# A gated cross-attention and MoE layer: two halves of the head stack, re-dealt and re-ordered

## The reference, cut to what matters

```python
# x, ctx: (32, 128, 128) f32; D = 128, H = 16 heads of DH = 8
q, k, v    = split_heads(layernorm(x) @ Wqkv + bqkv)
_, ka, va  = split_heads(ctx @ Wqkv_aux + bqkv_aux)
p  = softmax(q @ k.T / sqrt(8));  pa = softmax(q @ ka.T / sqrt(8))
out = (p @ v) * (1 - sigmoid(g)) + (pa @ va) * sigmoid(g)      # per head
x = x + tanh(g_xattn) * (merge_heads(out) @ Wo + bo)
# then a mixture of 64 experts, 8 chosen per token, and a shared one
x = x + tanh(g_ffn) * moe(layernorm(x))
```

## Time and profile before

| | |
|---|---|
| median of the runs | 859.26 us |
| the profiled execution: time, span | 859.58 us, 857.8 us |
| PE, DVE, ACT, POOL busy, share of the span | 96%, 80%, 66%, 74% |
| attention, start to the first block | 0 to 36.4 us |
| attention, blocks | 36.4 to about 289 us |
| experts | about 289 us to the end |

### The profile page before, as it was taken

How to read it: one execution, slowest core, us unless ns; L and a number is a source line. 1 busy time by engine, 2 the same in 40 slices (tenths; PEclk the granted TensorE clock), 3 DMA queues, 4 the chain that set the end, 5 groups by cost and what they waited for, 6 DMA issues and landing times.

```text
span 857.8 us, 20206 instructions
## 1 busy us (share of the span) xinstructions
PE 826.2 (96%) x6733; PEld 646.0 (75%) x6733; DVE 683.6 (80%) x1648; ACT 566.8 (66%) x964; POOL 637.3 (74%) x602
## 2 busy tenths in 40 slices
PE   4899999999999999999999999999999999999997
PEld 3477777777766678888888888878888888888885
DVE  6789999999897769769678877867966977876665
ACT  4388888888878665575576576557557557655554
POOL 2668888888854378877787786777777788778785
PEclk8599999999999999999999999999999999999999
DMA  4677786776652167447456554654654755546562
GB/s 119 173 169 173 178 183 155 187 169 170 160 126 51 53 152 169 120 111 184 117 142 147 131 142 125 154 135 109 163 139 111 171 130 134 149 116 150 137 138 58
DMA packets 108036, 120.04 MB, mean 140 GB/s; under 512 B 28560, under 2 KB 70352, under 8 KB 106496
## 3 DMA queue, kind: packets, MB, share of 16 engines
q1 hardware_dynamic: 105056, 118.23, 57.5%
q10 hardware_dynamic: 2880, 0.59, 0.4%
HBM read 103.55 MB, written 14.71 MB: 138 GB/s over the span
## 4 chain that ended last, share of the span: by engine, by line
PE 87%; DVE 5%; DMA 3%; issue 2%; SPq 1%; ACT 1%; POOL 0%; DVEq 0%; POOLq 0%
PE bank L1999 20%; PE bank L2000 20%; PE bank L2001 20%; PE bank L1336 7%; PE bank L1323 5%; PE bank L1294 3%; PE bank L1276 2%; PE bank L1344 2%; PE bank L1260 1%; PE bank L1357 1%; DVE mx L989 1%; PE bank L1270 1%; DMA cwb<-wts_scratch 1%; DMA stack_q<-nmaxT 1%; PE bank L1976 1%
## 5 line engine op out<-in xcount | busy, mean ns | idle before, releaser
L1676 POOL TENSOR_TENSOR hid<-act,cwb 128x512 f32<-128x512 f32 x264 | 424.0, 1615 | 126.4 <-DVE act L1903 69.1
L1729 ACT ACTIVATE silu<-bank 128x512 f32<-128x512 f32 x256 | 152.9, 597 | 190.7 <-PE bank L2001 189.9
L1903 DVE TENSOR_TENSOR act<-silu,bank 128x512 f32<-128x512 f32 (+1 forms) x264 | 180.5, 684 | 119.5 <-ACT silu L1729 78.7
L1999 PE MATMUL bank<-xhi,weights_hi 128*128 128x512 f32 x520 | 206.6, 397 | 0.0
L1911 DVE TENSOR_TENSOR hlo<-hid,hhi 128x512 fp32r<-128x512 f32 x256 | 197.5, 772 | 8.5 <-ACT hhi L1735 8.3
L2001 PE MATMUL bank<-xlo,weights_hi 128*128 128x512 f32 x520 | 204.2, 393 | 0.0
L2000 PE MATMUL bank<-xhi,weights_lo 128*128 128x512 f32 x520 | 203.9, 392 | 0.0
L1735 ACT ACTIVATE hhi<-hid 128x512 fp32r<-128x512 f32 (+1 forms) x264 | 164.8, 625 | 15.7 <-POOL hid L1676 13.1
L989 DVE TENSOR_REDUCE mx<-bank 128x4 f32<-128x512 f32 x240 | 156.0, 683 | 16.6 <-PE bank L1294 14.8
L786 ACT ACTIVATE prob<-bank 128x1024 f32<-128x1024 f32 x128 | 131.2, 1025 | 48.6 <-PE bank L1323 46.5
L2001 PEld LDWEIGHTS bank<-xlo,weights_hi 128*128 128x128 f32 x520 | 97.6, 188 | 22.0
(11 more groups left out here) (238 smaller groups left out, 1022.1 us busy)
## 6 DMA issues: line engine op xcount, KB each, us to landing
cwb<-wts_scratch SPq DMA_DIRECT2D x174, 384.0 KB, 5.4
stack_k<-k_scratch SPq DMA_DIRECT2D x30, 256.0 KB, 4.3
k_scratch<-parts_k SPq DMA_DIRECT2D x15, 384.0 KB, 3.4
stack_q<-q_scratch SPq DMA_DIRECT2D x30, 128.0 KB, 2.9
stack_k<-k_scratch SPq DMA_DIRECT2D x30, 128.0 KB, 5.2
q_scratch<-parts_q SPq DMA_DIRECT2D x15, 192.0 KB, 2.7
xin<-in_x_dram SPq DMA_DIRECT2D x16, 128.0 KB, 3.0
cin<-in_ctx_dram SPq DMA_DIRECT2D x16, 128.0 KB, 3.1
```

The lines of the kernel that those rows point to most:

```text
L1676: pool.tensor_tensor(h_buf[k][:], a_buf[k][:], cwb[slot][:, q % GP, :], ALU.mult).then_inc(h_ok, 1)
L1729: act.activation(s_buf[k % RS][:], g_bank[k % 2][:], ACT.Silu).then_inc(s_ok, 1)
L1903: nc.vector.tensor_tensor(a_buf[k % RS][at], s_buf[k % RS][at], u_bank[k % 3][at], ALU.mult).then_inc(a_ok, 1)
L1999: nc.tensor.matmul(bank, w[0], mh, start=first, stop=False)
```

## The change

Even heads go into half 0 and odd heads into half 1. The columns of the weights and biases are put in that order by ScalarE (`by_row`); the biases are now loaded as rows by two plain DMAs, re-ordered by three one-row copies on ScalarE, turned into columns by three one-column matmuls (`turn_biases`) and copied out by ScalarE. In a round PE issues the eight shifted products first, neighbours in opposite halves, then the four score products, neighbours in opposite halves again. `st_mm` is raised twice, by the last two shifted products. `stack_there` waits for both halves, once, in round 0. The first scores and maxima are dealt in the same way.

```diff
-S_HEAD = (8, 10, 12, 14, 0, 2, 4, 6)
+S_ROW = (0, 8, 2, 10, 4, 12, 6, 14)
+ROW_OF = tuple(h % 2 * (H // 2) + h // 2 for h in range(H))
...
-        turned = lambda a: a.rearrange("(h d a) -> d h a", d=DH, a=1)
-        for i, b in enumerate((turned(v["bqkv"][0:P]), turned(v["bqkv"][P:2 * P]), turned(v["bqkv_aux"][P:2 * P]))):
-            sp.dma_start(bcol[:, i:i + 1], b, allow_slow_non_contiguous=True).then_inc(c_in, 16)
+        sp.dma_start(brow_in[:, 0:2 * P], one(v["bqkv"][0:2 * P])).then_inc(c_in, 16)
+        sp.dma_start(brow_in[:, 2 * P:3 * P], one(v["bqkv_aux"][P:2 * P])).then_inc(c_in, 16)
...
+        act.wait_ge(c_in, 16 * 2)
+        for i in range(3):
+            act.activation(brow[:, i * P:(i + 1) * P].rearrange("a (d f i) -> a d f i", d=DH, f=2),
+                           brow_in[:, i * P:(i + 1) * P].rearrange("a (i f d) -> a d f i", d=DH, f=2),
+                           ACT.Copy).then_inc(b_row, 1)
...
         evac_t(0, 0)
+        act.wait_ge(b_mm, 1)
+        act.activation(bcol[:], st_bank[0][:, 0:3], ACT.Copy).then_inc(b_ev, 1)
...
-        def stack_there(b, u):
+        def stack_there(b):
             n, c, s = b // CH, b % CH, b // CH % NST
             if c == 0:
-                wait(pe, stk[S_HEAD[u] // HH][s], 64 * ((n - 1) // NST + 1 if s else n // NST))
-            if u == 0:
-                wait(pe, shift_zero, CH if n == NST else b - CH * NST + 1)
+                for half in (1, 0):
+                    wait(pe, stk[half][s], 64 * ((n - 1) // NST + 1 if s else n // NST))
+            wait(pe, shift_zero, CH if n == NST else b - CH * NST + 1)
...
-            a, h = u % 2, (u // 2) * HPU + j
+            a, h = u % 2, ROW_OF[(u // 2) * HPU + j]
...
-            ins = nc.tensor.matmul(st_bank[u % 2][:, j * P:(j + 1) * P], k_of(n)[at, h % HH, c, a, :],
+            at_p = (a * 2 + j // 2) * P
+            ins = nc.tensor.matmul(st_bank[j % 2][:, at_p:at_p + P], k_of(n)[at, h % HH, c, a, :],
                                    q_of(n)[at, h % HH, c, :], start=True, stop=True)
-            if j == HPU - 1:
+            if a == 1 and j >= 2:
                 ins.then_inc(st_mm, 1)
...
+        def turn_biases():
+            pe.wait_ge(b_row, 3)
+            pe.wait_ge(kones_ok, 4)
+            for i in range(3):
+                ins = nc.tensor.matmul(st_bank[0][:, i:i + 1], brow[:, i * P:(i + 1) * P], ones[0:1, 0:1],
+                                       start=True, stop=True)
+            ins.then_inc(b_mm, 1)
...
-                    if two_more and r % 2 == 0:
-                        stack_there(b + 2, 2 * r)
-                    for u in (2 * r, 2 * r + 1):
-                        ahead = (b + 2, u) if two_more else None
-                        shifted(b, u, 0)
-                        if ahead:
-                            scores(*ahead, 0)
-                        shifted(b, u, 1)
-                        shifted(b, u, 2)
-                        if ahead:
-                            scores(*ahead, 1)
-                        shifted(b, u, 3)
+                    if two_more and r == 0:
+                        stack_there(b + 2)
+                    u0, u1 = 2 * r, 2 * r + 1
+                    for u in (u0, u1):
+                        for j in range(HPU):
+                            shifted(b, u, j)
+                    if two_more:
+                        for j in range(2):
+                            scores(b + 2, u0, j)
+                            scores(b + 2, u1, j)
```

More of the change, by code:

```diff
@@ L227, in attention @@
     prob = [m(f"prob{i}", [P, 2, HPU * P], F32) for i in range(RP)]
+    brow, brow_in = (prob[0][0:1, k, 0:3 * P] for k in range(2))
     mx = [m(f"mx{i}", [P, 4, HH], F32) for i in range(2)]
@@ L722, in on_act, with by_row @@
         act.activation(warm[:], zero[:], ACT.Exp).then_inc(warm_ok, 1)
[L724 to L725 removed]
+        def by_row(to, w):
+            act.activation(to.rearrange("p (d f i) -> p d f i", d=DH, f=2),
+                           w.rearrange("p (i f d) -> p d f i", d=DH, f=2), ACT.Copy).then_inc(wqk_ok, 1)
         act.wait_ge(w_qkv_in, 32)
[L727 to L729 removed]
+        by_row(wqk[:, 0, :], wqkv[:, 0, :])
+        by_row(wqk[:, 1, :], wqkv[:, 1, :])
+        by_row(wqk[:, 2, :], wqkva[:, 1, :])
+        act.wait_ge(c_in, 16 * 2)
[3 more added lines that the diff above has]
+                           ACT.Copy).then_inc(b_row, 1)
         def clear_stack_q(i):
@@ L995, in first_maxima @@
             wait(dve, s_mm, 2 * (pair + 1))
-            f, h = S_HEAD[2 * r] // HH, S_HEAD[2 * r] % HH
-            nc.vector.tensor_reduce(mx[b][:, 2 * f:2 * f + 2, h:h + 4].rearrange("p a h -> p h a"),
-                                    (wide, two_banks)[pair % 2][:].rearrange("p (h a k) -> p h a k", h=4, a=2),
+            h = S_ROW[2 * r]
+            nc.vector.tensor_reduce(mx[b][:, :, h:h + 2].rearrange("p (f a) h -> p f h a", f=2),
+                                    (wide, two_banks)[pair % 2][:].rearrange("p (f h a k) -> p f h a k", f=2, h=2, a=2),
                                     AXX, ALU.max).then_inc(mx_ok, 2)
@@ L1301, in first_scores @@
             wait(pe, mx_ok, 2 * (pair - 1))
-            for u in (2 * r, 2 * r + 1):
-                for j in range(2):
-                    h = S_HEAD[u] + j
-                    if j == 0 and u in (0, 4):
-                        wait(pe, stk0[h // HH][b], 64)
+            if r == 0:
+                for half in (1, 0):
+                    wait(pe, stk0[half][b], 64)
+            for j in range(2):
+                for u in (2 * r, 2 * r + 1):
+                    h = S_ROW[u] + j
                     at = slice(*SCORE_ROWS[h // HH])
@@ L1400, in on_pe @@
         transposes(0, 0)
+        turn_biases()
         pe.wait_ge(wqk_ok, 3)
```

15 lines of the change are left out of this document (6 added, 9 removed).

## The result

The changed kernel takes 863.16 us (median of 6, 861.89 to 865.12), the kernel before 859.25 on the same chip: ratio 1.0046, 95% interval 1.0035 to 1.0058. That is +3.9 us where +7.1 was forecast. Spans are 857.8 us before and 861.5 after.

What follows compares the result with a forecast made beforehand. PE, VectorE, ScalarE and DMA were all taken as close to limiting. Passes +1.4, start +2.2, clock +0.3, chunk waits +2.9, bias 0, end +0.3 gave +7.1: 866.4 us, range 859.5 to 872 (likeliest case 861.5 to 870).

Steps and rivals of the forecast that it cites:

- those that end at or under 860.2: Exponential decides, key loads in time: 857.9 us, chance 0.12; gains and losses cancel, stack waits 1 us: 860.2, chance 0.09.
- Exponential released earlier: Exponential starts 0.45 us after its block instead of 0.68; -0.15 and -0.08 in a pass of eight rounds.
- Pairs: Neighbouring products in opposite halves: same columns to stream, weight loads already overlap in today's blocks; taken as 0.
- rival with hidden loads: Three same-half neighbours per block cost 0.094 us each today; 128 blocks give back 36 us, so 830; chance 0.01.
- that of serial pairs: Pairs don't run side by side; half of them serial adds 0.22 us in 128 rounds, so 894; chance 0.04.
- Maxima and the chain behind them: Later scores delay maxima, VectorE's copy and ScalarE's queue without slack: +0.30 and +0.04 a pass; net pass +0.11, 13 passes +1.4.
- Start: At chunk 1, waiting for half 0's last key load puts the first block at 38.59 instead of 36.43: +2.2 us.
- clock's +0.3: After the later first block, a shorter burst may raise the clock one step later: +0.3 us, bounds 0 and 1.2.
- Chunks 2 to 15: First blocks of six of fourteen chunks wait for half 0's keys: +2.9 us carried through, lower bound 0, worst 5.0.
- End: Last eight rounds 0, as VectorE sets the end; 241 to 274 us costs +0.3, bounds -1 and +2.
- Bias path: Row copies fit ScalarE's idle time, column matmuls lie in the wait for `xcT`: 0, bounds -0.2 and +0.3.
- VectorE becomes the bound: Every pass +0.27 or more, stack waits stay at 4, stretch to 274 us gives +2: 872 us; chance 0.12.

Runs made afterwards that it cites:

- e1: Kernel before, with only the wait for both stack halves moved into round 0, ahead of all products: 862.93 us, ratio 1.0039.
- e7: Kernel before, with the wait for half 0 in round 1 instead of round 2: 858.38 us, ratio 0.9987.
- e12: Second run of the kernel before with the wait for half 0 in round 1 instead of round 2: 858.81 us, ratio 0.9995.
- e6: Changed kernel, with shift_rows of odd elements issued in round 1 instead of round 0: 864.03 us, ratio 1.005.
- e2: Changed kernel, with each exponential held back until its round's scores are done: 864.97 us, ratio 1.0056.
- e3: Changed kernel, with SyncE issuing the key loads before the expert weights: 874.69 us, ratio 1.0166.
- e8: Changed kernel, with the four score products ahead of the eight shifted ones: 865.42 us, ratio 1.0065.
- e11: Kernel before, with half 0's wait in round 1 instead of 2 and shift_rows of odd elements in round 1: 859.85 us, ratio 1.0006.
- e10: Kernel before, with only the change's bias path (row loads, row copies, one-column matmuls): 860.16 us, ratio 1.0004.
- e5: Changed kernel, with the wait for both halves moved behind the eight shifted products: 861.97 us, ratio 1.0028.
- e9: Changed kernel, with the wait behind the eight shifted products and shift_rows of odd elements in round 1: 861.84 us, ratio 1.0032.
- e4: Kernel before, with the new order inside a round alone, heads dealt to the halves as before: 879.96 us, ratio 1.0235.

## Why the prediction was right, and where its sizes were off

The time, 863.2 us, lies in the forecast's own range of 861.5 to 870, in its lower part: the waits for the loads decide, as it said. Of the rivals, those that end at or under 860.2 needed these waits to shrink to 1.4 us or less, and they are 2.3 behind a start that is 1.9 later.

*Exponential released earlier: the size right, its cause only in part.* It starts 0.46 after its block. The period before the block that the earlier trace rows has at 151.02 falls from 1.88 to between 1.74 and 1.76, the one before 154.79 from 1.85 to 1.76: forecast -0.15 and -0.08, measured -0.13 and -0.09. But e1, e7 and e12 get 1.79 at the first of these with the late exponential, by having no wait of its own for half 0 there. The change takes this second `stack_there` away too, and the prediction counted that as nothing. With the wait gone, the earlier exponential adds only 0.04 there (1.79 to 1.75); what it would give with the wait still there no run shows. So that this term came out to 0.02 is in part luck.

*Pairs: right at 0.* No block pays for the loads. The rival with hidden loads and that of serial pairs are both out. The Trainium skill ("TensorE: Matmul & The Clock Gate", Part 3) had a weight load overlap a matmul only in another row group; the trace of before already spoke against it, and a round that gave back three loads isn't seen here either.

*Maxima and the chain behind them: the mis-sized term.* The copy and the DMA issue are 0.30 later after their block, as forecast. The step that failed is "None of this has slack". The exponential at 157.67 in the earlier trace rows seemed to be released by `full_q`, which ends at 157.68. But 157.67 is also the release by the shifted products of its own block (156.99, plus 0.40 to the last one, plus 0.28). In the changed kernel the next exponential starts at 160.28, 0.10 before `full_q` ends at 160.38: that is how close it follows. So `full_q` was 0.09 away from being the limit before, and +0.30 became +0.21. With +0.02 elsewhere, a pass comes to +0.01, not +0.11; 13 passes to +0.1, not +1.4.

A second limit stands right behind this one, and the prediction didn't see it at this block: the scores behind 159.39 wait for the maxima, which costs PE 0.18. Without any exponential PE's own work would bring the next block at 161.28 (160.71 + 0.64 - 0.07), the exponential brings it at 161.35. That is why e6, which frees the exponential, wins 0.07 a pass (15.60 to 15.53) and not 0.20. The prediction had checked this wait for a round whose maxima start at 0.65 ("just not late"), and then followed only the copy and ScalarE's queue in the round where VectorE has 1.01 us of other work in front.

*Start: right.* First block at 38.34 for 38.6 forecast, waiting for a `stack_k` load. One profile is a weak basis: after, e2, e3, e6 and e8 have the same program up to the first block, except e3's and e8's order of issue, and mean 38.76; before, e7, e11 and e12 mean 36.39. That is +2.4 for +2.2. The clock's +0.3 is not shown. From block 0 to block 8 after has 16.7 us, before 16.8 and e10 16.6, but e6 has 17.2, e1 17.4 and e2 17.8; and so have e7 and e11 (17.3) and e12 (17.6), which start like the kernel before. Most of this difference, up to 1.2 us, lies in when the products reach the pace of the higher level, with the old kernel's start and with the new one, and no profile ties it to the later first block.

*Chunks 2 to 15: right in kind.* Waits for keys of 2.9 us were forecast, and there are 2.3; the rest as a whole grew by 2.5. Which chunks was guessed badly: 4 and 12 hit, 8, 10 and 11 named and not waiting for keys, 5 and 9 not foreseen. e1 shows that the wait for both halves makes the kernel slower with all else left alone; in e5, where it stands behind the shifted products, the time is 1.2 us lower, with intervals that just overlap.

*End: wrong sign, 0.9 us.* The argument was that pairing "halves their 0.44 us, but the end is VectorE's: 0". Block 120 to block 127 takes 12.16 to 12.18 us in all kernels with the new deal (after, e2, e3, e5, e6, e8, e9) and 12.57 to 12.59 in all with the old, e4 with the new order among them. So these 0.41 us are the deal's. The first five of the seven periods shrink, from 8.90 us in sum to 8.12. The sixth grows, from 1.92 to 2.29, and there VectorE does bound: the weighted products wait for its `residual` (L1049), which stands behind the routing. They start 0.10 behind its end (in the kernel before 0.11, 284.04 against 283.93):

```profile
287.49 0.34 DVE L1049 SCALAR_TENSOR_TENSOR x<-bank,tg_x,xin 128x128 f32<-128x128 f32 x1
```

```profile
287.93 0.64 PE L1350 MATMUL bank<-prob,V 128*32 128x128 f32 x16 [0.57 <-issue]
```

So VectorE takes back half of what the pairs give, and not all of it. That PE waits for an exponential in this stage, and not for VectorE, could have been read at the block of before that follows 273.80; VectorE's share of busy time (14.1 of 16) was taken for a limit of every round instead.

*Bias path: 0*, as e10 has it within its interval.

The difference to the forecast is 3.2 us: by this profile (which comes to 3.3) 1.3 from the pass, 0.4 from the waits of chunks, 0.9 from the end, 0.7 from start and clock (2.5 forecast, 1.8 here; the scatter of starts may be all of the last). The rival "VectorE becomes the bound" did not occur as a whole: a pass grew by 0.01 and not by 0.27. In one round of eight VectorE is a limit, though (0.18 at the scores), and e8 shows that it isn't far in the others.

Left open: why the DMA chains of different chunks land up to 1.4 us apart from profile to profile, and with it how the rest divides between the chunks; and when the clock leaves the lower level at the start.

## To carry to other kernels

A re-ordering that frees one engine earlier is worth what the next release in the pass lets through, here 0.05 us a pass by e2; what it asks for sooner (the second half of a load, 2 us later than the first) cost several times that. Where two candidates could have released an instruction at the same time, compute both; the one that is not named is the slack. And when a late link is freed and the gain is small, look for the next limit in the same round: here the scores' own wait for the maxima stood 0.07 us behind the exponential.
A wait is best put right in front of the first instruction that needs it, or at a block that waits for nothing else late; and a load order that looks wrong (weights ahead of keys) may be what keeps the head of a long chain of transfers free.

## What the runs showed of the hardware that was not expected

*Products in different row halves start out of the program's order* (e4: 187.01 ahead of 187.06, 187.11 and 187.17). The Trainium skill ("TensorE: Matmul & The Clock Gate", Part 3) calls matmuls strictly ordered in start and end; these rows disagree, at least in their starts. Their ends are modelled.

*The granted clock in the profile can be wrong at the start.* The window from 38.30 in the changed kernel shows 1.00, but its first block takes 0.61 for the eight shifted products, and a block from 43.40 on 0.40. The same 0.61 stands at 41.34. That is the pace of the lower level, 1.2 GHz; by 42.83, where sixteen weighted products take 0.64 as everywhere later, it is over. In e6 the rows are as slow, and the window from 41.60 to 42.40 shows 0.50. In the kernel before the clock had left this level at 39.8, in the middle of its second block. In e12, which starts 0.4 us sooner, the eight shifted products are as slow at 39.00 as at the start.

*A wait of its own that is already fulfilled costs 0.09 us in front of a block that follows an exponential, and nothing in front of one that follows PE's own work.* A pass is 15.50 in e1, e7, e11 and e12, and 15.59 in before and e10. In e7, e11 and e12 the wait is still there, in front of round 1 instead of round 2.

*A wait of PE can cost more than its own length.* In e3 PE is busy 0.2 of the 2.3 us from 118.50 to 120.77, the granted clock then goes to 0.50 for 6.8 us, and the round behind costs 2.6 us on top of the wait. In the changed kernel the longest wait behind the start, 1.3 us at chunk 9, is followed by no such stretch. In e8 one of 3.4 us follows a wait of 1.7 us. That the wait is what lowers the clock is read from this order in three places and was not tried apart.
